# Layer one's edge sums: one product of 256 columns per slot in place of two of 128

## The reference

```
feat      = relu(x @ W[o] + b[o])             # o = 0 own, o = 1 neighbour; 4 heads of 32
att_s     = leaky(feat[0] . a_self)           # per node and head
att_n     = leaky(feat[1] . a_neigh)
edge_w    = (att_s[row] + att_n[col]) * adj_vals
agg[row] += edge_w * feat[1][col]             # over the edges
feat      = normalise feat[0], agg per head; scale, offset
x1        = layernorm(x + concat(feat))
```

## Time and profile before

| | us |
|---|---|
| median of 3 runs | 4674.34 |
| lowest, highest | 4673.16, 4681.0 |
| the profiled execution | 4711.94 |
| its span, first to last instruction | 4709.9 |

### The profile page before, as it was taken

The page is one execution under the profiler, slowest core; times in us unless marked ns, Lnnn a source line. Parts: engine busy times, 40 slices in busy tenths (PEclk is TensorE's granted clock), DMA queues, the critical chain, the costliest instruction groups (busy, mean ns, idle before and its releaser), DMA issues.

```text
span 4709.9 us, 91356 instructions
## 1 busy us (share of the span) xinstructions
PE 4022.3 (85%) x29127; PEld 3492.7 (74%) x29127; DVE 3424.2 (73%) x7577; ACT 2773.3 (59%) x7171; POOL 2682.8 (57%) x2816
## 2 busy tenths in 40 slices
PE   3999999989999999997678778778787787787776
PEld 3999999989999999996456666656566665666655
DVE  7787888878888888885566666666666666666666
ACT  3666777766666666664455555555555555555554
POOL 3665777734444444443666666666666666666662
PEclk9999999999999999999799889888888898898888
DMA  3555444455666666664455455555555545555554
GB/s 115 176 181 181 160 161 161 163 188 180 188 192 186 183 187 192 189 185 142 128 148 149 145 149 151 151 147 147 146 148 149 153 144 146 151 149 147 146 147 89
DMA packets 362447, 746.15 MB, mean 158 GB/s; under 512 B 59379, under 2 KB 189757, under 8 KB 361945
## 3 DMA queue, kind: packets, MB, share of 16 engines
q0 software_dynamic: 113952, 357.63, 27.3%
q1 hardware_dynamic: 248025, 382.64, 24.4%
HBM read 548.22 MB, written 193.43 MB: 157 GB/s over the span
## 4 chain that ended last, share of the span: by engine, by line
PE 69%; DVE 11%; another core or an unknown queue 9%; issue 6%; DVEq 2%; ACT 1%; DMA 1%; POOL 0%; SPq 0%; ACTq 0%; POOLq 0%
PE ps L1247 12%; PE ps L1258 10%; PE ps L1224 10%; PE ps L1225 9%; PE ps L1076 9%; DVE big L1765 6%; PE ps L1206 4%; DVE arena L1775 3%; PE ps L1066 2%; PE ps L1082 2%; PE ps L1136 2%; PE ps L1278 2%; PE ps L1106 2%; PE ps L1147 2%
## 5 line engine op out<-in xcount | busy, mean ns | idle before, releaser
L751 POOL DMA_INDIRECT arena<-d_p,tabs x1628 | 1559.6, 958 | 911.5 <-issue 474.1
L1247 PE MATMUL ps<-arena 128*128 128x256 f32 x3256 | 922.2, 424 | 248.4 <-DVE big L1765 186.3
L1258 PE MATMUL ps<-big,scr 128*128 x3256 | 865.1, 406 | 314.1 <-DVE arena L1775 223.7
L1775 DVE TENSOR_TENSOR arena<-arena,ps 128x512 f32<-128x512 f32 x814 | 533.5, 684 | 769.4 <-remote 474.6
L1034 ACT ACTIVATE arena<-arena 128x1024 f32<-128x1024 f32 x407 | 430.1, 1057 | 1068.0 <-DVE arena L1775 913.6
L1258 PEld LDWEIGHTS ps<-big,scr 128*128 128x128 f32 x3256 | 657.9, 205 | 457.3 <-issue 357.5
L1247 PEld LDWEIGHTS ps<-arena 128*128 128x128 f32 x3256 | 646.4, 208 | 455.5 <-ACT arena L1034 222.0
L737 POOL DMA_INDIRECT arena<-d_m,scr x392 | 507.1, 1294 | 701.7 <-PE ps L1225 525.1
L1765 DVE SCALAR_TENSOR_TENSOR big<-big,tabs,ps 128x256 f32 x1628 | 776.0, 477 | 108.7 <-DVE big L1765 51.9
L1224 PE MATMUL ps<-arena,scr 128*128 128x128 f32 x3920 | 771.6, 279 | 2.0 <-DVE arena L1621 2.0
L923 ACT ACTIVATE arena<-arena 128x128 f32<-128x128 f32 x1960 | 607.0, 390 | 25.1 <-DMA arena<-d_m,scr 24.7
(11 more groups left out here) (278 smaller groups left out, 6057.7 us busy)
## 6 DMA issues: line engine op xcount, KB each, us to landing
arena<-d_loc SPq DMA_DIRECT2D x407, 256.0 KB
d_m<-arena SPq DMA_DIRECT2D x108, 603.0 KB, 2.9
d_m<-arena SPq DMA_DIRECT2D x108, 469.0 KB
arena<-d_p,tabs POOLq DMA_INDIRECT x1628
arena<-in_xT_dram SPq DMA_DIRECT2D x96, 256.0 KB, 3.8
d_xp<-arena SPq DMA_DIRECT2D x49, 256.0 KB
arena<-d_xp SPq DMA_DIRECT2D x49, 256.0 KB
d_x<-arena SPq DMA_DIRECT2D x49, 256.0 KB
```

Of the source, the lines that this page charges most:

```text
L751: e.indirect_dma_start(out=G1[j % 8][:, k, :], out_offset=None, in_=d_p, in_offset=bass.IndirectOffsetOnAxis(ap=tabS[:, j, k:k + 1], axis= ...
L1247: m = e.matmul(turn(H, AB)[:, k * 256:k * 256 + 256], OH1[(j - 2) % 4][:, 2 * h + k, :], G1[(j - 2) % 8][:, 2 * h + k, :], start=True, sto ...
L1258: m = e.matmul(turn(H, QB)[:, k * 256:k * 256 + 256], OT1[j % 2][:, 2 * h + k, :], big[:, ts[2 * h + k] + 1, :], start=True, stop=True)
L1775: e.tensor_tensor(v, v, q2(turn(2 * j + h, QB)[:, :]), ALU.add).then_inc(S("f_m"), 1)
```

## The change

Features are no longer weighed in place. ACT writes them to the left half of a row of 256 in a new ring `SW` of three, DVE writes the gated ones to the right half, and PE sums both halves with one product of 256 columns per slot. The gather ring has four buffers instead of six, and a gather waits for DVE's product of piece g-4 in place of PE's of piece g-6. Weighing piece g now also waits until PE has finished piece g-3. In the changed kernel the lines from 921 on move down by one, those from 1225 to 1621 stand as before, and those from 1622 on move down by one.

```diff
-AW = 12032
+AW = 12160
...
-SHARED.update({f"f_g{g + 4}": (f"e_g{g}", 16 * ((NGA - g + 5) // 6)) for g in range(4)})
+SHARED.update({f"f_g{g + 4}": (f"e_g{g}", 16 * ((NGA - g + 3) // 4)) for g in range(4)})
...
-        GB = [take(PIECE, RW) for _ in range(6)]
+        GB = [take(PIECE, RW) for _ in range(4)]
...
-        UW = [take(PIECE, 128)]
-        take(8192 - 7732)
+        SW = [take(PIECE, 256) for _ in range(2)]
+        take(8320 - 8312)
...
-        UW += [take(PIECE, 128) for _ in range(2)]
+        SW.append(take(PIECE, 256))
...
-                waitn(e, "e_d", g - 5)
-                e.indirect_dma_start(out=GB[g % 6].rearrange("p a b -> p (a b)"), out_offset=None, in_=runs_m,
+                waitn(e, "e_u", g - 3)
+                e.indirect_dma_start(out=GB[g % 4].rearrange("p a b -> p (a b)"), out_offset=None, in_=runs_m,
...
             def weigh(g):
-                waitn(e, f"e_g{g % 6}", 16 * (g // 6 + 1))
+                waitn(e, f"e_g{g % 4}", 16 * (g // 4 + 1))
+                waitn(e, "e_d", g - 2)
                 for s in range(PIECE):
-                    v = GB[g % 6][:, s, :]
-                    a = e.activation(v[:, 0:128], v[:, 0:128], ACT.Copy, scale=v[:, FW + 1:FW + 2])
+                    v = GB[g % 4][:, s, :]
+                    a = e.activation(SW[g % 3][:, s, 0:128], v[:, 0:128], ACT.Copy, scale=v[:, FW + 1:FW + 2])
...
-                    e.matmul(AC(p)[:, h, 0:128], OHW[g % 3][:, s, :], GB[g % 6][:, s, 0:128], start=first, stop=False)
-                    m = e.matmul(AC(p)[:, h, 128:256], OHW[g % 3][:, s, :], UW[g % 3][:, s, :], start=False, stop=end)
+                    m = e.matmul(AC(p)[:, h, :], OHW[g % 3][:, s, :], SW[g % 3][:, s, :], start=first, stop=end)
...
-                e.tensor_tensor(UW[g % 3].rearrange("p s (h d) -> p s h d", h=4), v[:, :, 0:128].rearrange("p s (h d) -> p s h d", h=4),
+                e.tensor_tensor(SW[g % 3][:, :, 128:256].rearrange("p s (h d) -> p s h d", h=4),
+                                SW[g % 3][:, :, 0:128].rearrange("p s (h d) -> p s h d", h=4),
```

More of the change, by code:

```diff
@@ L735, in gath0 @@
                 waitn(e, "e_ti", t + 1)
-                waitn(e, "e_d", g - 5)
-                e.indirect_dma_start(out=GB[g % 6].rearrange("p a b -> p (a b)"), out_offset=None, in_=runs_m,
-                                     in_offset=bass.IndirectOffsetOnAxis(ap=TI[:, t, i:i + 1], axis=1)).then_inc(S(f"e_g{g % 6}"), 16)
+                waitn(e, "e_u", g - 3)
+                e.indirect_dma_start(out=GB[g % 4].rearrange("p a b -> p (a b)"), out_offset=None, in_=runs_m,
+                                     in_offset=bass.IndirectOffsetOnAxis(ap=TI[:, t, i:i + 1], axis=1)).then_inc(S(f"e_g{g % 4}"), 16)
             for g in range(NGA):
@@ L1613, in ready @@
             def ready(g):
-                v, t, b5 = GB[g % 6], g // NQ, [128, PIECE, 128]
-                waitn(e, f"e_g{g % 6}", 16 * (g // 6 + 1))
+                v, t, b5 = GB[g % 4], g // NQ, [128, PIECE, 128]
+                waitn(e, f"e_g{g % 4}", 16 * (g // 4 + 1))
                 waitn(e, "e_d", g - 2)
@@ L1676, in node @@
                 if o == 0:
-                    waitn(e, "e_d", 8 * (p + 1))
+                    waitn(e, "e_d", 2 * NQ * (p + 1))
                     waitn(e, "d_as", p + 1)
```

## The result

| | before | changed |
|---|---|---|
| median of 6 runs, us | 4673.75 | 4649.65 |
| lowest, highest | 4667.16, 4681.0 | 4645.42, 4654.97 |
| profiled execution, its span | 4711.94, 4709.9 | 4649.49, 4647.9 |
| edge stage, first to last start of an edge record | 1205.9 | 1180.1 |
| a round of eight pieces in the middle | 24.65 | 24.06 |

The ratio is 0.9951, with a 95% interval of 0.9938 to 0.9964: 23 us faster, between 17 and 29. The medians differ by 24.1. The forecast was 29 us less (4645.5, range 4638 to 4660), so the measured 4649.65 lies within the range, 4 us above the likeliest value.

What follows compares the result with a forecast made beforehand. The prediction took PE's own work to bound layer one's edge stage. Wider products save 29 us, weight loads, ACT's wait and gathers cost 0, so the median of 4674.34 becomes 4645.5 us, range 4638 to 4660.

Steps and rivals of the forecast that it cites:

- The bound: Layer one's edge stage, 980.9 to 2187.0 us: PE busy 1205.27 of 1206.10 us, so shortening PE's work shortens the kernel.
- The products: Edge products on PE: one of 256 columns per slot takes 0.4312 us instead of 0.446, saving 29 us over 1960 slots.
- L1206's 0.0135: Lower bound per slot, from L1206's eight records in the edge stage at 0.4325 us per product: 26 us saved.
- upper bound of 34 us: Edge products: 5 us more if pieces no longer lose the extra 0.1 us after a narrow product; not counted.
- rival 1: Edge products: wide records losing 0.1 us more at three shape changes a round give back 15 us, 4660; chance 0.10.
- The weight loads: Edge products' loads on PE: half go, 7840 records to 3920, but they run beside the products; nothing counted.
- ACT's wait: Weighing on ACT waits for PE's g-3, DVE up to 2.0 us a round, PE never; cost 0.
- the fill at 980 us and the tail to 2260 us keep their work: Start and end of the edge stage: work unchanged, listed among the parts that cost nothing.
- rival 2: Edge stage: ACT's held weighing delays node work, DVE becomes the bound; 4704 just past break-even, up to 4826; chance 0.04.
- leads of 3.1 us and above: Edge stage: DVE's products end 3.1 and 4.4 us before PE takes them, so a 0.7 us delay leaves over 2.
- The gathers: Four buffers, released by DVE's product of g-4: issued 0.6 us sooner, nobody on the path waits; cost 0, no gain.
- The sum: Whole kernel: 29 us less than the median of 4674.34, giving 4645.5 us, 0.6% less.

Runs made afterwards that it cites:

- two-products run: Changed kernel, but each slot summed as two products of 128 columns: 4331.06 us against 4326.32 for the kernel before, ratio 1.0008.
- the run with 64 and 192 columns: Changed kernel, but each slot summed as products of 64 and 192 columns: 4518.77 us in one run, against 4326.32 for the kernel before.
- ring of four: Changed kernel with four SW buffers, weighing waiting for PE's piece g-4: 0.9923 of the kernel before, 0.9935 when timed again.
- The wait alone: Kernel before plus only the wait of weighing piece g until PE has finished g-3: 4325.99 us against 4326.32, ratio 1.0002.
- the pair: Kernel before and changed kernel as first measured, chip not on record: 4649.65 us against 4673.75, ratio 0.9951.
- the two repetitions: Unaltered changed kernel timed again against the kernel before: 4301.92 us against 4327.35 (0.9943), and 4297.16 against 4328.18 (0.9933).

## Why the prediction was right, and what it missed

**The bound** was read rightly. PE stays busy throughout the stage, before and after, and the two-products run shows that nothing else in the change makes the kernel faster.

**The products.** Forecast 0.0148 us per slot, 0.59 per round; measured 27.36 us over 46 steady rounds (1127.97 to 1100.61), 0.595 per round. Taking layer two's longest unbroken stretch as the price was right to the hundredth, and L1206's 0.0135 was the lower bound it was taken for. A piece behind L1062 still loses the 0.1 us that it lost before (1467.63 to 1469.89, 2.26 us against 2.16), no less and no more, so neither the upper bound of 34 us nor rival 1 came true.

**The weight loads** were said to cost nothing, "what little they cost is within the spacings". For the sum that holds. As a picture it was incomplete: the run with 64 and 192 columns shows a floor of 0.112 us for a record that another load follows, and at 128 columns the records, 0.112 apart, already stand on it. A record of 192 costs 0.163 and one of 256 0.216, so 64 columns cost 0.053; by this 128 columns would be 0.110 without a floor. Of the 0.0148 per slot, some 4 x 0.002 = 0.008 may thus be the floor and the rest the four gaps that became two. This is an estimate from rounded spacings, and only the floor itself was shown. By it, part of the gain is that of rarer loads, which the prediction put at nothing; its sum was right because it took the spacing of wide records whole, loads included.

**ACT's wait** went as worked out in the steady rounds: ACT held nearly every time, DVE by at most 0.8 us (0.5 and 0.7 forecast) and about 1.1 us a round (2.0 forecast), PE never.

**The step that failed** is the sentence "the fill at 980 us and the tail to 2260 us keep their work", with the cost of **0** for ACT's wait in all 49 rounds. They keep their work, but the last rounds don't keep their cover. 49 rounds at 0.595 would be 29.2 us; the stage got 25.8 us shorter. The first round is 0.7 us shorter, with 0.5 us less at the lower clock; the next 46 are 27.4 us shorter; and the last sixteen pieces are 2.3 us longer (56.64 against 54.37), where they should be 1.2 shorter. These 3.5 us go as follows:

- With the ring of four the same sixteen pieces take 53.32 us, 1.05 less than before. The longer ring thus gives back 3.3 of the 3.5 us.
- The wait alone, in the kernel before, costs 2.5 us there. The rest is mainly the dip of the clock behind PE's longer wait, 0.75 us.

The mechanism is that of rival 2, ACT's node work behind a held weighing. But it reaches PE by a path that the prediction didn't look at. Its leads of 3.1 us and above were those of DVE's product over PE's edge product, which keeps at least 1.0 us in hand to the end, before and after. What ran out is the lead of ACT's normalisation over PE's transposes. In the middle round before it is 5.5 us, from the end of L963 (1467.60) to the start of L1197:

```profile
1466.52 1.08 ACT L963 ACTIVATE arena<-arena,small 128x256 f32<-128x256 f32 x2
```
```profile
1473.13 0.60 PE L1197 MATMUL ps<-cstb,arena 128*128 128x128 f32 x4
```

In the last full round it was nothing even before the change: PE waited 0.20 us there, and waits 2.10 now.

**The gathers** were rightly priced at nothing: with them and two products of 128 the whole time is 1.0008 of the kernel before.

**The sum**: 29 us were forecast. The profiles of the pair show 25.8 in the edge stage, 3.5 less than 49 steady rounds would give. The medians of the whole differ by 24.1 in the pair, and by 25.4 and 31.0 in the two repetitions; these three differ by no more than their scatter. The stretch between the last edge product and layer two varied between 31.8 and 38.9 us over all the profiles, and no run ties it to the change.

## What to carry to other kernels

An f32 product should be wide enough that its records are longer than the loads of its weights (0.216 us against 0.11 here). Two products with the same weights belong side by side in one buffer, even if that costs a ring and a wait. Before adding a wait on an engine that works in order, measure the lead in the tightest round of the stage and not in a typical one, and for everything that the critical engine waits for. Here the edge products had 3 us in hand in a steady round and the transposes 5.5, while in the hurried last one PE already waited 0.2 us for the latter. A new wait of the critical engine can cost more than its length: here 0.75 us more, at the lower clock that followed. And when two profiled executions differ by more than the medians do, compare the stage that was changed, whose length here repeats to 0.1%, before explaining the whole.

## What the runs showed of the hardware that was not expected

- A 128x64 f32 product with 128 x 128 weights, followed by one of 192 columns with the same weights, costs as much as a 128x128 one, about 0.112 us per record (two records per product), within 0.1 us per round of what that floor gives (28.72 against 28.7). The weight loads start 0.110 us apart at the least.
- After 2.10 us in which PE stood still, the granted clock was 0.50 for 3.4 us in the middle of a stage that otherwise ran at 1.00, in all three profiles of the changed kernel; after 1.96 us at the same place in another variant it stayed at 1.00.
- The same kernel takes 4674 us in the runs of the pair and 4327 us on three chips of the variants. The edge stage of layer one, bound by PE at a clock of 1.00, is the same within 2 us. What follows it is 346 us shorter on those chips. Layer two of the changed kernel, in the pair:

```profile
2260.00:4640.00 2380.00, 1862.60 (x7490) 1450.81 (x7489) 1547.08 (x3588) 1304.45 (x2833) 1516.23 (x1580) 0.91 0.53 148
```

  and on chip 10:

```profile
2260.00:4280.00 2020.00, 1749.18 (x7353) 1355.50 (x7352) 1509.46 (x3529) 1281.35 (x2786) 1513.58 (x1569) 0.97 0.61 172
```

  PE is idle about 520 us in the one and 270 in the other, at a clock of 0.91 and 0.97 and at 148 and 172 GB/s. Which of these is the cause and which follows from it was not tried.
